# A two-layer attention kernel: GpSimd takes over VectorE's half of the low-part subtractions

## What is computed

```python
h = tokens(x) + positions                      # 29 features -> 128
h = h + attn0(layernorm(h))                    # group norm, 8 heads of 64, softmax over 1024 keys
h = h + ffn0(layernorm(h))                     # triangular token-channel product, gelu, product
h = h + attn1(layernorm(h))                    # 8 heads of 16
h = h + switch(layernorm(h))                   # 16 experts, one per token, with a capacity
```

## Time and profile before

| | |
|---|---|
| runs, median (lowest to highest) | 7491.77 us (7490.42 to 7492.68) |
| profiled execution, its own time | 7493.21 us |
| its span, first to last instruction | 7491.4 us |
| mean granted TensorE clock | 0.915 of full speed |
| busy: TensorE (PE) | 6426.3 us, 86% |
| VectorE (DVE) | 4993.9 us, 67% |
| ScalarE (ACT) | 3176.8 us, 42% |
| GpSimd (POOL) | 1774.5 us, 24% |

### The profile page before, as it was taken

How to read it: one execution, slowest core, us unless ns; L and a number is a source line. 1 busy time by engine, 2 the same in 40 slices (tenths; PEclk the granted TensorE clock), 3 DMA queues, 4 the chain that set the end, 5 groups by cost and what they waited for, 6 DMA issues and landing times.

```text
span 7491.4 us, 124439 instructions
## 1 busy us (share of the span) xinstructions
PE 6426.3 (86%) x39399; PEld 4048.6 (54%) x39399; DVE 4993.9 (67%) x11546; ACT 3176.8 (42%) x6291; POOL 1774.5 (24%) x1623
## 2 busy tenths in 40 slices
PE   6798897988989899898997989889898897988976
PEld 4565554555555455554654545555555554555543
DVE  5576776757767576675766757667676776767664
ACT  2354443444434344343443434444344443444431
POOL 2323222222222222222222222222222222222200
PEclk8899898998989899898998989989899998999987
DMA  2121211112112111211212112121110211211100
GB/s 62 39 64 22 66 33 48 43 31 50 34 47 43 45 41 30 53 43 39 43 25 55 43 37 43 25 55 43 43 41 22 66 33 48 43 32 48 36 27 8
DMA packets 91264, 308.93 MB, mean 41 GB/s; under 512 B 27030, under 2 KB 32102, under 8 KB 80358
## 3 DMA queue, kind: packets, MB, share of 16 engines
q1 hardware_dynamic: 90598, 300.55, 17.4%
HBM read 49.33 MB, written 41.94 MB: 12 GB/s over the span
## 4 chain that ended last, share of the span: by engine, by line
issue 62%; POOL 19%; PE 13%; DVE 5%; DMA 1%; POOLq 1%; SPq 0%; ACT 0%; DVEq 0%; ACTq 0%
POOL pr_lo L457 10%; POOL on L1188 3%; PE bank L754 2%; POOL on L1180 2%; PE bank L781 2%; PE bank L740 2%; DVE hm L1454 1%; PE bank L779 1%; PE bank L811 1%; DVE mxh L1464 1%; PE bank L797 1%; PE bank L798 1%; DMA stacks<-parts 1%; POOL h L1158 1%; POOL rs L1155 1%
## 5 line engine op out<-in xcount | busy, mean ns | idle before, releaser
L1464 DVE TENSOR_REDUCE mxh<-bank 128x1 f32<-128x512 f32 x4096 | 2759.2, 688 | 1512.6 <-PE bank L754 1480.5
L1034 ACT ACTIVATE pr<-bank 128x512 f32<-128x512 f32 x4096 | 2396.5, 598 | 2651.6 <-PE bank L781 2613.8
L754 PE MATMUL bank<-stacks 128*128 128x512 f32 x4096 | 1859.1, 459 | 479.9 <-DVE mxh L1464 404.5
L781 PE MATMUL bank<-stacks 65*128 65x512 f32 (+1 forms) x4096 | 1961.5, 480 | 9.2 <-ACT pr L1034 7.6
L754 PEld LDWEIGHTS bank<-stacks 128*128 128x128 f32 x4096 | 835.0, 204 | 1108.1 <-DVE mxh L1464 837.2
L457 POOL TENSOR_TENSOR pr_lo<-pr 128x1024 bf16<-128x1024 f32 x496 | 940.1, 1895 | 1917.1 <-ACT pr L1034 1917.1
L797 PE MATMUL bank<-v,pr 128*128 128x129 bf16 x8192 | 1075.4, 224 | 7.8 <-DVE pr_lo L457 5.4
L779 PE MATMUL bank<-stacks 128*128 128x512 f32 x2048 | 1030.8, 503 | 47.4 <-issue 41.1
L798 PE MATMUL bank<-v,pr_lo 128*128 128x129 bf16 x7936 | 1021.6, 222 | 0.0
L781 PEld LDWEIGHTS bank<-stacks 65*128 65x128 f32 (+1 forms) x4096 | 817.3, 200 | 334.4 <-issue 185.8
L797 PEld LDWEIGHTS bank<-v,pr 128*128 128x128 bf16 x8192 | 792.4, 100 | 268.3 <-issue 252.1
(11 more groups left out here) (181 smaller groups left out, 5079.7 us busy)
## 6 DMA issues: line engine op xcount, KB each, us to landing
stacks<-parts SPq DMA_DIRECT2D x384, 512.0 KB, 6.8
parts_d<-pr SPq DMA_DIRECT2D x16, 2048.0 KB, 6.5
stacks<-parts_d SPq DMA_DIRECT2D x224, 128.0 KB, 3.0
stacks<-parts_d SPq DMA_DIRECT2D x224, 64.0 KB, 2.7
stacks<-mrow SPq DMA_DIRECT2D x512, 2.0 KB
out<-hm SPq DMA_DIRECT2D x16, 512.0 KB, 2.7
stacks<-pr SPq DMA_DIRECT2D x32, 128.0 KB, 5.9
stacks<-pr SPq DMA_DIRECT2D x32, 64.0 KB, 3.7
```

What stands on the lines that cost most here:

```text
L754: mm(maxb[k % 2][:, :], qs[:, t * P:(t + 1) * P], ks[:, g * HALF:(g + 1) * HALF], start=True, stop=True).then_inc(max_filled.sem, 1)
L781: mm(bank[:, :], k_stack(layer, head)[0:last, kk], q_stack(layer, head)[0:last, q], start=(layer == 1), stop=True).then_inc(score_filled.s ...
L1034: act.activation(pr[:, at % 2, kt, :], score[k % 2][:, :], ACT.Exp, scale=SCALES[layer]).then_inc(exp_done.sem, 1)
L1464: dve.tensor_reduce(mxh[:, layer, n // 2, n % 2:n % 2 + 1], maxb[k % 2][:, :], AX_X, ALU.max)\
```

## The change

GpSimd makes all four pairs of a unit. Pair 1 moves into its program at step 4, pair 3 at step 0 of the following unit (in first, after the last unit, at the start of `serial`). VectorE makes none. The two semaphores become one.

```diff
-        lo_done = Counts(sem("lo_done"), 16 * (4 - len(POOL_PAIRS)))
-        lo_pool = Counts(sem("lo_pool"), 16 * len(POOL_PAIRS))
+        lo_done = Counts(sem("lo_done"), 16 * 4)
...
                 if j == 0:
-                    te.wait_ge(lo_done.sem, lo_done.at(seg.l0, (u + 1) * (4 - len(POOL_PAIRS))))
-                    te.wait_ge(lo_pool.sem, lo_pool.at(seg.l0, (u + 1) * len(POOL_PAIRS)))
+                    te.wait_ge(lo_done.sem, lo_done.at(seg.l0, 4 * (u + 1)))
...
             def attention(seg, *beside):                      # GpSimd
                 for step, at, layer, u, kt in steps_of(seg.kind):
-                    if layer == 0 and kt in LO_STEPS and (kt - 1) // 2 in POOL_PAIRS:
-                        lo_parts(pool, seg, at, kt - 1).then_inc(lo_pool.sem, 1)
+                    if layer == 0 and kt in LO_STEPS:
+                        lo_parts(pool, seg, at, kt - 1).then_inc(lo_done.sem, 1)
+                    elif kt == 0 and at > 0 and units_of(seg.kind)[at - 1][0] == 0:
+                        lo_parts(pool, seg, at - 1, T - 1).then_inc(lo_done.sem, 1)
...
             def serial(seg):                                  # GpSimd
                 at = len(units_of(seg.kind)) - 1
+                if seg.kind == "first":
+                    lo_parts(pool, seg, at, T - 1).then_inc(lo_done.sem, 1)
...
-            def lo_pair(seg, at, kt):                         # VectorE
-                if kt // 2 not in POOL_PAIRS:
-                    lo_parts(dve, seg, at, kt).then_inc(lo_done.sem, 1)
...
             def attention(seg, *beside):                      # VectorE
                 for step, at, layer, u, kt in steps_of(seg.kind):
-                    if layer == 0 and kt in LO_STEPS:
-                        lo_pair(seg, at, kt - 1)
-                    elif kt == 0 and at > 0 and units_of(seg.kind)[at - 1][0] == 0:
-                        lo_pair(seg, at - 1, T - 1)
...
             def serial(seg):                                  # VectorE
-                if seg.kind == "first":
-                    lo_pair(seg, at, T - 1)
...
-POOL_PAIRS = (0, 2)
```

## The result

The changed kernel takes 7615.72 us (median of four runs, 7611.4 to 7621.51), the kernel before 7491.1 us beside it (four runs, 7479.58 to 7492.68): a ratio of 1.017, 95% interval 1.0153 to 1.0188. It is 125 us slower; the forecast was 76 us slower. The profiled execution is one of 7621.51 us, span 7619.7 us, against the span of 7491.4 us before: 128 us to be found in the trace.

The account below looks back on a forecast made before the run. TensorE waits for a unit's last pair, so when it is ready and who makes it decides. Terms 26 + 3 + 2 + 14 + 16 + 22 = 83, less some 7, gave 76 us slower: 7568 us, range 7512 to 7640.

Parts of the forecast that it names:

- L1188 would cost 0.29 us: GpSimd's `normalize1` ahead of pair 3: falls from 1.20 to 0.29 us once VectorE's subtraction no longer holds GpSimd off.
- The rival that it keeps 1.20 us: L1188 stays long, so some 238 units are each 0.91 us later, 217 us: 7785; chance 4%.
- Usual units 0.17 us late: Pair 3 on GpSimd lets TensorE start at 503.62 instead of 503.45; over 154 units, 26 us.
- Pair 1 hidden in a usual unit: VectorE's 1.22 us there lie in its idle time, GpSimd's 1.89 us fit between pairs 0 and 2: no gain.
- 1.58 us late before unit 2: GpSimd's pair 1 holds VectorE's L1433 in 14 switch-layer segments: 22 us; bounds -0.5 and +1.9 us each.
- Unit 0: In 14 switch-layer segments GpSimd's pair 2 holds VectorE's L1322, which ends 1.15 us late: 16 us.
- the first collision: Unit 0: only pair 2 holds L1322, since VectorE's instruction has then waited longer than pair 3; 1.15 us.
- the upper bound of 3.1: Unit 0: lateness of L1322 in us if pair 3 goes first as well, 1.89 us more.
- Unit 15: In 15 segments, with no maxima to wait for, pair 3 makes TensorE start 0.92 us late: 14 us.
- the part on the clock: TensorE's 2.4 GHz stays in usual units; in units 0 and 2, bounds of nothing and 42 us for more 1.2 GHz.
- the other rivals: Besides L1188 staying long: faster, 7469, chance 6%; and no change that shows, within 0.2% or 15 us, 7506, chance 10%.
- the faster rival: Units 0, 1 and 2 of 14 segments: VectorE wins both collisions and its backlog shrinks, 23 us faster, 7469; chance 6%.

Follow-up runs that it names:

- that without the collisions: The changed kernel, but in loop and penult VectorE keeps pairs 1 and 3 of unit 0 and pair 1 of unit 2: 7558.31 us, ratio 1.0092.
- the pair 1 kernel: Against the kernel before, only pair 1 moves to GpSimd and pair 3 stays on VectorE: 7536.84 us, ratio 1.0068.

## Why the prediction was right where it was, and what it mis-sized

**L1188 would cost 0.29 us** once VectorE's subtraction is gone: right, 292 to 295 ns in all 256. The rival that it keeps 1.20 us is out. The Trainium skill, SBUF — State Buffer, section Who interferes with whom, calls the pair of ports that VectorE and GpSimd share an exclusive lock, for which a VectorE instruction with two SBUF inputs contends with a GpSimd instruction that reads SBUF. The trace agrees, with this and with the 1.87 us of L1435.

**Usual units 0.17 us late**: 0.15 at the start of the products in the unit of the rows, +0.22 from exponential to exponential in the loop. That the row of units 1 to 14 comes out at 21 us against 26 is luck. It holds a gain that I had not counted: in units 7 and 11 the clock had fallen to 1.2 GHz before (51 and 68 us at the low clock over the 13 turns), and after the change it doesn't fall there at all. Together they are 25 us shorter; the others are 46 us longer. TensorE idles more there than before, 2.0 us a unit where it was 1.1 and 1.4, and still keeps its clock. In first it is the same: the late units are late (0.3 us each, the last 2.8), but 10 us less at the low clock turn +5 into -3.

**Pair 1 hidden in a usual unit, and 1.58 us late before unit 2**: right, 1.60 us measured in the stretch (14.08 to 15.68 us). In the trace with pair 1 alone the collisions are 37 us.

**Unit 0**: the place and the mechanism were right. The step that failed is "I take the first collision alone, since VectorE's instruction has then waited longer than pair 3". The first collision was priced rightly: with pair 1 alone it is 1.16 us against 1.15. But in the changed kernel pair 3 gets ahead of VectorE's z in all 14 segments. Where pair 2 holds the first z as well, in seven, the eighth z ends 2.75 us late, near the upper bound of 3.1. In the other seven it ends 1.3 to 1.5 us late. The mean is 2.1, some 30 of the 35 us against 16; the rest goes with a longer time at the low clock, which I had as a bound. Held instructions count as busy, so VectorE's busy time shows it too: it fell by 514 us and not by some 620, with the z of the switch segments 32 us longer in all, L1435 16 us.

**Unit 15**: the lateness was right, 0.99 us against 0.92, and its price was wrong: 43 us against 14. The step that failed is in the part on the clock: "the gap of a usual unit moves but keeps its 1.2 us, so the clock stays". I had read that from stretches behind the gap of a usual unit, and did not ask it of unit 15, whose gap grows from 0.35 to 1.33 us. There the clock fell (61 us at the low clock over the 13 turns, none before), 2.9 us for each 0.99. The experiment with these fifteen subtractions alone, 57 us, shows the price. The stretches between the segments, for which I had nothing, grew by 14 us there as well as in the change. But in the kernel with pair 3 ahead of the scaling in units 1 to 14, which leaves unit 15 alone, they grew by 17, so that these us are unit 15's isn't shown.

**Slower against the other rivals.** The gain from VectorE's backlog, on which the faster rival stood, is small: GpSimd wins both collisions. Without any collision the change is still 0.9% slower. The total, 125 us against 76, is thus two terms too small by 48 us (unit 0 and unit 15) and one that was missing, 14 us, less some 10 us elsewhere.

**What stays open.** Which gap makes the clock fall can't be told from these traces ahead of a run: with the same 1.92 us in unit 4 it fell in twelve of thirteen turns of one kernel and in seven of thirteen of another. So the give-back in units 7 and 11 and the falls in units 15 and 4 of kernels that didn't touch them are read from the records of the clock, not derived. Where the extra us between the segments come from is open. So is the stop of VectorE by 0.2 to 0.4 us at a fixed instruction: it comes once a turn in the changed kernel (ahead of L1489, 0.31 us, in unit 10), at one to three places in six of the seven experiments, and neither in the kernel before nor in that without the collisions. Together with the clock it moved some 24 us in one experiment, so differences of that size between two kernels can't be given to the moved subtractions without the trace.

## What to carry to other kernels

When the last item of a batch is what an in-order engine waits for, look at what stands ahead of it in the program of the engine that makes it: moving pair 3 in units 1 to 14 to GpSimd cost 64 us with the scaling ahead of it (some 24 of them in unit 4, by another cause) and gained 151 us with the scaling behind it; the whole change went from 125 us lost to 116 gained by the same step. Price a delay where it lies: 0.15 us late cost 0.2 us in a usual unit, while 0.99 us late in unit 15 came with the low clock and cost 2.9 us. And leave an idle engine idle at the few places where it would hold off another engine's urgent work; here that is 3 of 64 subtractions of a segment, worth some 55 us.

## What the runs showed of the hardware that I had not expected

GpSimd and VectorE take turns at their exclusion by single instructions, not by who has waited: after pair 2 one z of VectorE ended, 1.80 us long instead of 0.34, then pair 3 ran for its whole 1.89 us and held the second z for 1.93, and only then, with nothing left queued on GpSimd, the six others ran at 0.34 us. That is read from the timeline of unit 0, where seven of 14 segments have this row; it wasn't tried by itself. TensorE's clock gave no simple rule. In unit 15 it fell in 13 of 13 turns with a gap of 1.0 to 1.3 us, in part before the gap, and in 7 of 13 of the pair 1 kernel with no gap above half a microsecond. In the usual units it stayed after 1.1 or 1.2 us (1.00 granted). After the same 1.92 us it did either, and keeping it was worth 1.6 us. And an engine can stop for 0.2 to 0.4 us at a fixed instruction of a program, waiting for nothing that the profile shows, at a place that differs from one version of the program to the next.
